# Splitting the carry product into four column tiles and re-ordering all engines' jobs in a fused attention and feed-forward block

## The reference, cut to what matters

```python
x = x + attn(cond(x, ids))             # per-sample 256x256 linear, then linear attention with
                                       # rotary features, gate, output product, layer norm
# cond2 on the new x:
ctx = causal_ema(x, tau_ctx)
gated = x * sigmoid(concat([x, ctx]) @ Wg.T + bg)
mod = 0.5 + sigmoid(gelu(x @ Wn1.T + bn1) @ Wn2.T + bn2)
traces = vmap(lambda tau, m: causal_ema(gated * m[..., None], tau))(tau_raws, moveaxis(mod, -1, 0))
temporal = einsum('dbtc,dc->btc', traces, softmax(blend, axis=0))
out = gelu(x @ Wsoma.T + bsoma) * sigmoid(temporal @ Wtemp.T + btemp)
y = layernorm(out @ Wout.T)
x = x + bitlinear(silu(bitlinear(y, w_gate)) * bitlinear(y, w_up), w_down)
```

## Time and profile before

| | us |
|---|---|
| median of 3 runs | 662.14 (659.56 to 666.24) |
| the profiled execution | 664.61 |
| its span, first to last instruction | 662.6 |
| PE busy in the span | 619.7 (94%) |
| DVE busy | 529.2 (80%) |
| POOL busy | 296.0 (45%) |
| ACT busy | 285.6 (43%) |
| mean granted TensorE clock | 0.974 of full |

### The profile page before, as it was taken

The page is one execution under the profiler, slowest core; times in us unless marked ns, Lnnn a source line. Parts: engine busy times, 40 slices in busy tenths (PEclk is TensorE's granted clock), DMA queues, the critical chain, the costliest instruction groups (busy, mean ns, idle before and its releaser), DMA issues.

```text
span 662.6 us, 17104 instructions
## 1 busy us (share of the span) xinstructions
PE 619.7 (94%) x6866; PEld 443.4 (67%) x6866; DVE 529.2 (80%) x1077; ACT 285.6 (43%) x597; POOL 296.0 (45%) x320
## 2 busy tenths in 40 slices
PE   8888989999999999999999999999998999998773
...
PEclk9897999999999999999999999999998999999876
...
DMA packets 81919, 52.84 MB, mean 80 GB/s; under 512 B 59058, under 2 KB 75698, under 8 KB 81330
## 3 DMA queue, kind: packets, MB, share of 16 engines
...
## 4 chain that ended last, share of the span: by engine, by line
PE 70%; DVE 15%; DMA 6%; POOL 5%; issue 3%; ACT 1%; SPq 0%; POOLq 0%; DVEq 0%
PE ps L484 63%; PE ps L487 7%; DVE B L902 3%; DVE EB L902 2%; DVE CT L1024 2%; DMA B<-g_rows 2%; DMA g_rows<-G 1%; DMA HQ<-HP 1%; DVE FT L911 1%; DVE HP L902 1%; DVE ZN L908 1%; DMA WQ<-wqkv 1%; POOL RS L1180 1%; POOL RS L1159 1%; POOL HP L1206 1%
## 5 line engine op out<-in xcount | busy, mean ns | idle before, releaser
L1180 POOL TENSOR_SCALAR RS<-MV,EPS 128x1 f32<-128x1 f32 x32 | 14.0, 439 | 211.0 <-DVE MV L1008 211.0
L902 DVE TENSOR_TENSOR B<-B,BLGS 128x1024 f32<-128x1024 f32 x64 | 92.5, 1487 | 4.3 <-DMA B<-g_rows 4.3
L484 PE MATMUL ps<-WQ,YT 128*128 128x512 f32 (+1 forms) x256 | 89.9, 493 | 1.4 <-DMA WQ<-wqkv 1.4
L902 DVE TENSOR_TENSOR EB<-ps,C 128x512 f32<-128x512 f32 x128 | 79.2, 680 | 8.2 <-PE ps L484 7.8
L484 PEld LDWEIGHTS ps<-WQ,YT 128*128 128x128 f32 x256 | 46.4, 190 | 37.6 <-issue 27.0
L484 PE MATMUL ps<-FW,ZQ 128*128 128x512 bf16 x256 | 62.7, 388 | 1.5 <-ACT ZQ L745 1.1
L745 ACT ACTIVATE FH<-ps,AM 128x512 f32<-128x512 f32 x64 | 43.5, 687 | 45.3 <-PE ps L484 42.0
L1206 POOL TENSOR_SCALAR HP<-HP,FT 128x1024 f32<-128x1024 f32 x32 | 39.0, 1220 | 51.9 <-DVE FT L905 51.7
L1159 POOL TENSOR_TENSOR KP<-TH,CS 128x512 f32<-128x512 f32 x32 | 44.0, 1377 | 32.0 <-ACT TH L745 17.5
L745 ACT ACT_TABLE_LOAD x41 | 52.6, 1283 | 2.3 <-PEq L1300 1.6
L902 DVE TENSOR_TENSOR HP<-FH,ps 128x512 f32<-128x512 f32 x64 | 42.0, 680 | 11.3 <-ACT FH L745 11.2
...
## 6 DMA issues: line engine op xcount, KB each, us to landing
...
```

The source lines that it names most:

```text
L484: return e0.matmul(o, l, r, start=start, stop=stop, skip_group_check=True)
L902: return e0.tensor_tensor(o, x, y, op)
L1180: e0.tensor_scalar(RS[:, s, 0:1], MV[:, s, 1:2], EPS[:, 0:1], None, ALU.add).then_inc(g["rs0"], 1)
```

## The change

Two things are changed. The carry product of `ema` is issued as four products of 32 output columns each in place of one of 128. And the HEAD, PERIOD and TAIL tables of all five engines are new; the period is run for ten `k` instead of eleven, with more in the head. The jobs themselves, their number and their waits stay as they are.

The core of the diff (PE, DVE and POOL periods, the heads in part; ACT's, SP's and the tails left out):

```diff
@@ PE_HEAD (in part) @@
-    ... ("e", 2), ("wsum", 1), ("cond", 2), ("cond", 3), ("xtr", 0), ("xtr", 1), ("o", 2), ("h1", 0), ("wg", 0), ("wg", 1), ("mod", 0),
+    ("cond", 0), ("proj", 0), ("qtr", 0), ("cond", 1), ("ktr", 0), ("proj", 1), ("low", 0), ("wsum", 0), ("e", 0), ("gate", 0),
+    ... ("e", 2), ("cond", 2), ("qtr", 3), ("xtr", 0), ("xtr", 1), ("o", 2), ("h1", 0), ("ktr", 3),
+    ("soma", 0), ("wsum", 2), ("wg", 0), ("e", 3), ("wo", 2), ("wg", 1), ("low", 2), ("o", 3), ("mod", 0), ("proj", 4), ("wo", 3),
@@ PE_PERIOD @@
-    ("ema", 2, -4), ("h1", 1, -1), ("soma", 1, -1), ("gate", 1, 0), ("o", 2, 0), ("ema", 2, -3), ("ktr", 2, 1), ("wg", 2, -2),
-    ("dn", 2, -8), ("wg", 2, -1), ("qtr", 2, 1), ("ztr", 2, -6), ("mod", 1, -1), ("ttr", 1, -2), ("wo", 2, 0), ("e", 2, 1),
-    ("proj", 2, 2), ("gu", 2, -6), ("ztr", 2, -5), ("temp", 1, -2), ("o", 2, 1), ("low", 1, 1), ("u", 1, -1), ("wo", 2, 1),
-    ("ktr", 2, 2), ("qtr", 2, 2), ("wsum", 1, 1), ("wout", 2, -4), ("wout", 2, -3), ("gu", 2, -5), ("xtr", 2, 0), ("dn", 2, -7),
-    ("cond", 1, 2), ("proj", 2, 3), ("xtr", 2, 1), ("e", 2, 2),
+    ("proj", 2, 3), ("xtr", 2, 1), ("gate", 1, 1), ("e", 2, 2), ("h1", 1, 0), ("ema", 2, -2), ("ema", 2, -1), ("o", 2, 2),
+    ("mod", 1, 0), ("dn", 2, -6), ("wg", 2, 0), ("qtr", 2, 3), ("wg", 2, 1), ("ztr", 2, -4), ("ztr", 2, -3), ("ktr", 2, 3),
+    ("wo", 2, 2), ("soma", 1, 0), ("ttr", 1, -1), ("e", 2, 3), ("gu", 2, -4), ("proj", 2, 4), ("temp", 1, -1), ("low", 1, 2),
+    ("o", 2, 3), ("u", 1, 0), ("gu", 2, -3), ("wo", 2, 3), ("cond", 1, 3), ("wout", 2, -2), ("wout", 2, -1), ("xtr", 2, 2),
+    ("dn", 2, -5), ("ktr", 2, 4), ("qtr", 2, 4),
@@ DVE_HEAD (in part) @@
-    ("og", 1), ("on", 0), ("wsc", 0), ("wred", 1), ("on", 1), ("em", 2), ("wsc", 1),
+    ("rq", 2), ("og", 0), ("wsc", 1), ("em", 1), ("on", 0), ("rq", 3), ("og", 1), ("on", 1), ("em", 2), ("wred", 2), ("ctx", 0),
+    ("tab2", 0), ("wsc", 2), ("wb", 0), ("em", 3), ("wb", 1), ("og", 2), ("modv", 0), ("gt", 0), ...
@@ DVE_PERIOD @@
-    ("tab2", 1, -2), ("ctx", 1, -2), ("zn", 1, -4), ("rq", 2, -1), ("tab1", 1, 1), ("fin", 2, -10), ("wb", 2, -4), ("wb", 2, -3),
-    ("modv", 1, -2), ("ae", 1, -2), ("gt", 1, -2), ("og", 2, -2), ("em", 2, -1), ("on", 2, -2), ("fs", 2, -8), ("sg", 1, -3),
-    ("rq", 2, 0), ("fr", 2, -8), ("og", 2, -1), ("tab0", 1, 1), ("ub", 1, -2), ("bn2", 1, -3), ("zc", 2, -6), ("on", 2, -1),
-    ("zc", 2, -5), ("wred", 1, 0), ("b4", 2, -4), ("fin", 2, -9), ("fs", 2, -7), ("wsc", 1, 0), ("fr", 2, -7), ("em", 2, 0),
-    ("rot", 1, 3), ("b4", 2, -3),
+    ("fr", 2, -5), ("b4", 2, -1), ("em", 2, 2), ("ctx", 1, 0), ("rq", 2, 3), ("zn", 1, -2), ("modv", 1, 0), ("wb", 2, 0),
+    ("fin", 2, -6), ("wb", 2, 1), ("gt", 1, 0), ("ae", 1, 0), ("og", 2, 2), ("em", 2, 3), ("on", 2, 2), ("rq", 2, 4), ("fs", 2, -4),
+    ("fr", 2, -4), ("b4", 2, 0), ("ub", 1, 0), ("sg", 1, -1), ("og", 2, 3), ("fs", 2, -3), ("on", 2, 3), ("bn2", 1, -1),
+    ("zc", 2, -2), ("fin", 2, -5), ("zc", 2, -1),
@@ POOL_HEAD @@
-    ("rk", 0), ("rk", 1), ("rk", 2), ("xb", 0), ("rs", 0), ("rs", 1), ("x1", 0), ("rk", 3), ("xb", 1), ("x1", 1), ("quant", 0),
-    ("quant", 1), ("rs", 2), ("xb", 2), ("xb", 3), ("x1", 2),
+    ("rk", 0), ("xb", 0), ("xb", 1), ("rk", 1), ("quant", 0), ("rk", 2), ("rs", 0), ("quant", 1), ("rs", 1), ("x1", 0), ("x1", 1),
+    ("xb", 2), ("rk", 3), ("xb", 3), ("quant", 2), ("rs", 2), ("x1", 2), ("rk", 4), ("rs", 3), ("x1", 3), ("ml", 0), ...
@@ POOL_PERIOD @@
-    ("rk", 2, 0), ("rs", 2, -1), ("x1", 2, -1), ("ml", 1, -2), ("xb", 2, 0), ("rs2", 1, -3), ("rk", 2, 1), ("quant", 1, 0),
-    ("hm", 2, -8), ("rs", 2, 0), ("hm", 2, -7), ("x1", 2, 0), ("xb", 2, 1),
+    ("x1", 2, 1), ("xb", 2, 2), ("hm", 2, -6), ("rs2", 1, -2), ("rk", 2, 3), ("rs", 2, 2), ("hm", 2, -5), ("x1", 2, 2),
+    ("xb", 2, 3), ("ml", 1, 0), ("rk", 2, 4), ("rs", 2, 3),
@@
-PERIODS = range(2, NU - 3)
+PERIODS = range(2, 12)
@@ ema @@
-                mm(bk[:, 0:256], PX[:, j * P:(j + 1) * P], UB[:, c // 4 % 2, :], False, True).then_inc(t["ema"], 1)
+                for r in range(0, P, 32):
+                    m = mm(bk[r:r + 32, 0:256], PX[:, j * P + r:j * P + r + 32], UB[:, c // 4 % 2, :], False, True)
+                m.then_inc(t["ema"], 1)
```

More of the change, by code:

```diff
@@ L38 @@
 PE_HEAD = (
[L39 to L42, removed]
@@ L43 @@
-    ("xtr", 2), ("ktr", 4), ("soma", 0), ("xtr", 3), ("e", 4), ("wsum", 2), ("low", 2),
+    ("cond", 0), ("proj", 0), ("qtr", 0), ("cond", 1), ("ktr", 0), ("proj", 1), ("low", 0), ("wsum", 0), ("e", 0), ("gate", 0),
+    ("proj", 2), ("o", 0), ("ktr", 1), ("qtr", 1), ("wsum", 1), ("wo", 0), ("e", 1), ("proj", 3), ("o", 1), ("low", 1), ("qtr", 2),
+    ("wo", 1), ("ktr", 2), ("gate", 1), ("e", 2), ("cond", 2), ("qtr", 3), ("xtr", 0), ("xtr", 1), ("o", 2), ("h1", 0), ("ktr", 3),
+    ("soma", 0), ("wsum", 2), ("wg", 0), ("e", 3), ("wo", 2), ("wg", 1), ("low", 2), ("o", 3), ("mod", 0), ("proj", 4), ("wo", 3),
@@ L44 @@
+    ("cond", 3), ("proj", 5), ("qtr", 4), ("xtr", 2), ("ktr", 4), ("xtr", 3), ("u", 0), ("gate", 2), ("e", 4), ("h1", 1), ("wg", 2),
+    ("wg", 3), ("soma", 1), ("ema", 0), ("o", 4), ("ema", 1), ("ktr", 5), ("qtr", 5), ("mod", 1), ("ttr", 0), ("wo", 4), ("e", 5),
+    ("proj", 6), ("temp", 0), ("o", 5), ("low", 3), ("u", 1), ("wo", 5), ("ktr", 6), ("qtr", 6), ("wout", 0), ("wout", 1),
+    ("xtr", 4), ("cond", 4),
 )
 PE_PERIOD = (
-    ("ema", 2, -4), ("h1", 1, -1), ("soma", 1, -1), ("gate", 1, 0), ("o", 2, 0), ("ema", 2, -3), ("ktr", 2, 1), ("wg", 2, -2),
@@ L54 @@
[L54 to L61, removed]
@@ L62 @@
-    ("wout", 2, -5), ("xtr", 2, -4), ("xtr", 2, -3), ("proj", 2, -1), ("h1", 1, -2), ("dn", 2, -10), ("gu", 2, -7), ("wg", 2, -4),
-    ("wg", 2, -3), ("mod", 1, -2), ("ztr", 2, -6), ("ktr", 2, -2), ("qtr", 2, -2), ("dn", 2, -9), ("gate", 1, -1), ("e", 2, -2),
[3 rows of a table removed]
-    ("wout", 2, -4), ("wout", 2, -3), ("dn", 2, -6), ("u", 1, -1), ("ztr", 2, -4), ("ztr", 2, -3), ("soma", 1, -1), ("gu", 2, -4),
-    ("ema", 2, -2), ("gu", 2, -3), ("ema", 2, -1), ("ttr", 1, -1), ("dn", 2, -5), ("temp", 1, -1), ("wout", 2, -2), ("wout", 2, -1),
@@ L69 @@
-    ("dn", 2, -4), ("dn", 2, -3), ("ztr", 2, -2), ("ztr", 2, -1), ("gu", 2, -2), ("gu", 2, -1), ("dn", 2, -2), ("dn", 2, -1),
+    ("proj", 2, -5), ("xtr", 2, -7), ("e", 2, -6), ("gate", 1, -3), ("low", 1, -2), ("ema", 2, -10), ("ema", 2, -9), ("h1", 1, -4),
+    ("soma", 1, -4), ("o", 2, -6), ("mod", 1, -4), ("dn", 2, -14), ("ktr", 2, -5), ("qtr", 2, -5), ("ztr", 2, -12), ("ttr", 1, -5),
+    ("wg", 2, -8), ("wg", 2, -7), ("e", 2, -5), ("temp", 1, -5), ("ztr", 2, -11), ("gu", 2, -12), ("wo", 2, -6), ("o", 2, -5),
@@ new lines @@
+    ("u", 1, -4), ("gu", 2, -11), ("proj", 2, -4), ("wo", 2, -5), ("cond", 1, -1), ("wout", 2, -10), ("ktr", 2, -4),
+    ("wout", 2, -9), ("qtr", 2, -4), ("dn", 2, -13), ("proj", 2, -3), ("gate", 1, -2), ("e", 2, -4), ("xtr", 2, -6), ("xtr", 2, -5),
+    ("dn", 2, -12), ("h1", 1, -3), ("ema", 2, -8), ("o", 2, -4), ("ema", 2, -7), ("mod", 1, -3), ("wg", 2, -6), ("wo", 2, -4),
+    ("ztr", 2, -10), ("ktr", 2, -3), ("wg", 2, -5), ("qtr", 2, -3), ("proj", 2, -2), ("e", 2, -3), ("gu", 2, -10), ("ttr", 1, -4),
@@ new lines @@
+    ("ztr", 2, -9), ("o", 2, -3), ("low", 1, -1), ("u", 1, -3), ("wo", 2, -3), ("soma", 1, -3), ("proj", 2, -1), ("temp", 1, -4),
+    ("ktr", 2, -2), ("gate", 1, -1), ("gu", 2, -9), ("qtr", 2, -2), ("dn", 2, -11), ("wout", 2, -8), ("wout", 2, -7), ("e", 2, -2),
+    ("xtr", 2, -4), ("xtr", 2, -3), ("ktr", 2, -1), ("ema", 2, -6), ("h1", 1, -2), ("o", 2, -2), ("qtr", 2, -1), ("wg", 2, -4),
[3 rows of a table added]
+    ("ema", 2, -4), ("mod", 1, -1), ("ema", 2, -3), ("dn", 2, -9), ("ttr", 1, -2), ("ztr", 2, -6), ("dn", 2, -8), ("gu", 2, -6),
```

17 lines of the change are left out of this document (10 added, 7 removed), and 122 rows, old and new, of tables (ACT_HEAD, ACT_PERIOD, ACT_TAIL, DVE_HEAD).

## The result

The changed kernel takes **630.87 us** (629.97 to 632.02, 4 runs) where the kernel before takes 663.25 beside it (659.56 to 666.24, 4 runs): ratio 0.9528, 95% interval 0.9482 to 0.9574, 4.7% less. The ratios and their intervals are worked out from the fast runs alone (in the second comparison four of the 17 runs of the kernel before are slow ones) and not from the medians, so the quotient of two medians can differ from them by some tenths of a per cent. The forecast was 637 with a range of 625 to 652.

> The changed kernel as it is, on the chip of the run beside it, as a second measure of the ratio of the two. Expected 0.953 by the first measure; if the distance between the two depends on the chip by more than 0.3%, the ratios of the other runs can't be laid side by side.

What follows compares the result with a forecast made beforehand. PE's own work was taken to bound the steady stretch, with PE waiting in head and tail. 662.6 - 11 - 6 - 8 = 637.6 for the span, 637 for the median; range 625 to 652.

Steps and rivals of the forecast that it cites:

- -11 was said: Steady stretch on PE: 39 fewer entries into small tiles save 12.1 us, less 1 for small-shape changes, net -11 us.
- The price of an excursion: PE: going from the full array into small tiles and back costs 0.09 + 0.11 + 0.11 = 0.31 us.
- a fixed overhead for each matmul: Split carry on PE: about 60 cycles per matmul would give back 4.8 us, making 642; the forecast took 0.
- the +1 for changes among small shapes: PE's new period: changes such as `o` into `mod` cost 0 to 0.1 us for 16, taken as 1 us.
- DVE below PE: Steady stretch: DVE needs 30.7 of 36.3 us a unit, 85%; steady loss 0 to 0.2 a unit, none in the centre.
- ring rival: Steady stretch: bank ring makes PE wait for DVE; slower kernel, 667 us (6%), or a smaller wait, 647 us (17%).
- -6 said: Head: new order removes stalls but a POOL rounding may show on PE; -6 us, bounds -12 and +6.5.
- the 8.0 of one place: Head, first `wg`: 4.9 us waiting for the scan plus 3.1 us at low clock, 8.0 us together.
- -8 said: Tail from `wo 31`: -10.6 of filled waits, +6 stretch, -3 RS, say -8 us; bounds -17 and +6.
- the RS term: Tail on POOL: the one-column RS operation takes 2.23 us, twice in the chain, mostly waiting; -3 us if that goes.
- the stretch: Tail behind `wo 31`: DVE's remaining work grows from 44 to 61 us, so the chain lengthens; +6 us.
- DVE has little less than its share in the steady stretch, so no gain: Old tail, 465 to 592 us, loses 10 us; DVE has 156.2 in 197 us, so no gain was taken.

Runs made afterwards that it cites:

- the kernel with the full carry: The changed kernel, new orders kept, with the carry product as one full-array product again: 638.52 us, ratio 0.9675 to the kernel before.
- the kernel with the split alone: The kernel before, all old orders kept, with only the carry product split into four column tiles: 656.66 us, ratio 0.995.
- when they are swapped: The changed kernel with `dn`, `gu`, `gu` each swapped with the f32 job behind it in PE's period: 634.64 us, ratio 0.9611 to the kernel before.
- the additions beside VectorE's SBUF operations: The changed kernel with five extra GpSimd additions a period, placed where VectorE reads two SBUF operands: 637.69 us, ratio 0.9675 to the kernel before.
- the same additions elsewhere: The changed kernel with five extra GpSimd additions a period, held until `modv` is done, when VectorE reads PSUM: 631.41 us, ratio 0.9557 to the kernel before.
- moving one job in the old table: The kernel before with `dn 19` moved behind `wg 25` in PE's tail table: 658.84 us, ratio 0.9969.

## Why the prediction was right, and where its steps were not

**Steady stretch: right in mechanism, two terms mis-sized.** -11 was said, -16 came. The price of an excursion, 0.31, holds (0.32 in the kernel with the full carry, and 0.38 a unit for one excursion in the kernel with the split alone). The split streams at no cost: 0.43 a set of four. That decides the weighing in the prediction against a fixed overhead for each matmul: eight records take the 0.43 of two, so the six more add nothing. Two terms were mis-sized. The way out of small tiles was priced 0.11 whatever follows; into the bf16 jobs it costs 0.01, and all three ways out of the new period lead into these (0.3 a unit, 0.42 with `u` when they are swapped). And the +1 for changes among small shapes is nothing: `o` into `mod` takes 322.04 to 322.92 = 0.88, with no surplus. Together they make a unit of 35.83 where 36.3 was said.

**DVE below PE: right for this kernel, and nearer the edge than the text says.** The unit is that of PE's own jobs, and no ring rival came true: PE's steady window has no gap. But the additions beside VectorE's SBUF operations took 7 us, the same additions elsewhere none. The prediction noted that B is stretched where GpSimd reads beside it and then left that out of the sum as hidden. In the changed kernel B's mean is 1314 ns against 1487 of before, 11 us of VectorE in all; with the mean put back to 1520 by the additions, the new order no longer covers it. So, as far as these two runs reach, the placing of GpSimd's operations brings no time of its own in the steady stretch; it is a condition under which the shape changes are paid out in full. The new orders with GpSimd's old placing were not run.

**Head: -6 said, -6.4 measured; the gain for the reason given, the loss from another place.** The wait before `wg 0` is 0.27 (under 2 was said), the scan 1.26, so the 8.0 of one place are gone. One link of the argument was idle: the scan's place ahead of `tab2` is worth 0.45 at `wg 0` and nothing later. PE waits for no KP or X behind the roundings. They are on the chain to `wg 0` all the same (rounding, load of the third weights, reduce, scan), and it ends just 0.27 behind PE. What took part of the 8.0 back is QP at 16.62 (4.03): PE's new head has `qtr 0` ahead of `cond 1` and `proj 1`, and QP begins only at 15.79, behind `tab0` on DVE, which waits for the load of W up to 13.92. Behind that wait PE is granted 0.50 of the clock from 16.7 to 20 us, and `cond 1` takes 17.50 to 20.91 = 3.41 where 1.73 is usual. The prediction's bounds covered this by number but not by name; that a guess between -12 and +6.5 came out within 0.4 is luck.

**Tail: -8 said, -11.8 measured, by two errors of opposite sign.** From `wo 31` to the end 73 to 75 was said, 79.5 came (548.74 to 628.2). Ahead of `wo 31` no gain was said; all 10 us came. By these two profiles, that is: 3.1 of the 10 are the slow transfer at `dn 19` and the low clock behind it, which the profile of the split alone does not have, and the second profile of the changed kernel takes 80.9 from `wo 31` to the end. Without these two pieces of chance the tail's gain is nearer 7 or 8 us than 12, and nearly all of it lies ahead of `wo 31`. PE in the tail of the changed kernel:

```profile
548.74 1.03 PE L492 MATMUL ps<-W,OT 128*128 128x256 f32 x4
...
555.69 0.44 PE L495 MATMUL ps<-C,X 128*128 128x128 f32 x2 [0.40 <-POOL X L1169]
...
591.57 1.07 PE L492 MATMUL ps<-B,ML 128*32 128x256 f32 x16 [0.77 <-DVE B L912]
...
623.41 1.89 PE L492 MATMUL ps<-FW,HQ 128*128 128x256 bf16 x8 [1.71 <-DMA HQ<-HP]
```

Following chunk 31 from stage to stage in both traces (starts on PE: `wo`, `xtr`, `ema`, `dn`) splits the 79.5:

| from, to | before | after | difference |
|---|---|---|---|
| `wo 31` to `xtr 31` | 591.95 to 602.18: 10.23 | 548.74 to 555.69: 6.95 | -3.3 |
| `xtr 31` to `ema 31` | to 626.24: 24.06 | to 591.57: 35.88 | +11.8 |
| `ema 31` to `dn 31` | to 657.86: 31.62 | to 623.41: 31.84 | +0.2 |
| `dn 31` to the end | 4.74 | 4.79 | 0 |

The first line is the RS term, said -3: the one-column operation takes 0.30 where it took 2.23 (and the one ahead of it 0.84). POOL in the changed kernel, for the earlier trace rows:

```profile
552.64 0.30 POOL L1190 TENSOR_SCALAR RS<-MV,EPS 128x1 f32<-128x1 f32 x1
```

The mis-sized term is the stretch: said 6, measured 11.8 + 0.2. It lies wholly between `xtr` and `ema`, where the jobs of earlier units were packed in. In those 35.9 us DVE is busy for 32.17, 90%, PE for 30.53. And the chain of waits of the changed kernel does not run through `wo 31` at all; it passes that time on unit 14's way (start, length, what):

```profile
554.06 3.40 DMA mod_rows<-MOD
...
557.54 3.26 DMA MODT<-mod_rows
...
564.15 2.33 POOL RS L1209
```

It began with unit 14's G on DVE (549.13) and goes on to TP (576.30), for which PE waits 2.35 at 577.02. So "the chain behind `wo 31`" was the wrong yardstick: by moving `wo 31` forward the new tail made an older chain the longest. The forecast's 6 was chosen between 0 and 17 (all of DVE's extra work) without a row that tells where in that range it lies; 17 less the waits that DVE had there would have been nearer.

Ahead of `wo 31` the step "DVE has little less than its share in the steady stretch, so no gain" failed. A share over 197 us says nothing about single waits: the waits there are local (2.80 or 1.10 for HQ, 1.40 for HP, 0.95 for ZN), and moving one job in the old table took 2 us out (0.1 to 4.0), as shown. That the new tail avoids the others for the same reason was not tried one by one; that they are gone is what the trace shows (PE has one wait of 0.27 us from 92 us to 555).
